# First attention block of a two-layer transformer kernel: order of the norm, the evictions, the value bias, the weight-chunk buffers and the bias row

## The reference, cut to what matters

```python
def _layernorm(x, axis=-1, eps=1e-05):
    m = jnp.mean(x, axis=axis, keepdims=True)
    v = jnp.var(x, axis=axis, keepdims=True)
    return (x - m) / jnp.sqrt(v + eps)

def _L0_attn_ref(x, Wqkv, bqkv, Wo, bo):      # x: 1 x 1024 x 512, d = 128
    qkv = jnp.einsum('bsc,cf->bsf', x, Wqkv) + bqkv
    q, k, v = ...                             # three parts of 128
    attn = jnp.einsum('bqd,bkd->bqk', q, k) / sqrt(d)
    attn = jax.nn.softmax(attn, axis=-1)
    out = jnp.einsum('bqk,bkd->bqd', attn, v)
    return jnp.einsum('bqd,dc->bqc', out, Wo) + bo

x = x + _L0_attn_ref(_layernorm(x), ...)
x = x + _L0_ffn_ref(_layernorm(x), w1, mean_w1, w2, mean_w2, w3, mean_w3)
```

## Time and profile before

| quantity | value |
|---|---|
| time, median of 3 runs | 1475.95 us (1475.61 to 1476.82) |
| time of the profiled execution | 1476.29 us |
| its span, first to last instruction | 1474.5 us |
| PE busy in the span | 1327.4 us (90%) |
| DVE, ACT, POOL busy | 1105.6 us (75%), 832.5 us (56%), 640.5 us (43%) |
| mean granted clock of PE | 0.954 |

### The profile page before, as it was taken

The page is one execution under the profiler, slowest core; times in us unless marked ns, Lnnn a source line. Parts: engine busy times, 40 slices in busy tenths (PEclk is TensorE's granted clock), DMA queues, the critical chain, the costliest instruction groups (busy, mean ns, idle before and its releaser), DMA issues.

```text
span 1474.5 us, 21228 instructions
## 1 busy us (share of the span) xinstructions
PE 1327.4 (90%) x7144; PEld 1105.3 (75%) x7144; DVE 1105.6 (75%) x2233; ACT 832.5 (56%) x1813; POOL 640.5 (43%) x629
## 2 busy tenths in 40 slices
PE   2777999999989789998659999999999999999977
PEld 1656788888789677776348888888888888888866
DVE  5637434433548599999969998898898998898864
ACT  4554442222236556774557767666676767667631
POOL 3421120000027445645556555655666555555522
PEclk9978999999999999998669999999999999999988
DMA  6531220000022334754820000000000000000101
GB/s 217 177 100 51 70 81 0 1 19 1 17 81 64 102 75 122 227 181 140 269 95 14 1 28 28 28 28 28 28 16 12 28 27 28 28 27 15 51 29 58
DMA packets 83722, 95.59 MB, mean 65 GB/s; under 512 B 11680, under 2 KB 59296, under 8 KB 83104
## 3 DMA queue, kind: packets, MB, share of 16 engines
q1 hardware_dynamic: 83616, 94.24, 20.2%
HBM read 75.34 MB, written 18.87 MB: 64 GB/s over the span
## 4 chain that ended last, share of the span: by engine, by line
PE 68%; DVE 18%; ACT 4%; issue 4%; DMA 2%; POOL 2%; SPq 1%; DVEq 1%; ACTq 0%; POOLq 0%
PE ps L328 16%; PE ps L330 15%; PE ps L329 15%; PE ps L1715 8%; PE ps L1735 3%; DVE acc L1299 3%; PE ps L1734 3%; DVE top L1310 2%; DVE xn_l L1361 1%; DVE rop L1322 1%; DVE acc L1313 1%; DVE rop L1320 1%; DVE pm L1349 1%; DVE rop L1321 1%; PE ps L1430 1%
## 5 line engine op out<-in xcount | busy, mean ns | idle before, releaser
L692 POOL TENSOR_SCALAR pm<-pm,smx 128x128 f32<-128x128 f32 (+7 forms) x256 | 190.5, 753 | 214.6 <-DVE smx L1355 214.6
L966 ACT ACTIVATE pm<-pm,smx 128x128 f32<-128x128 f32 (+7 forms) x256 | 197.2, 772 | 39.8 <-DVE smx L1349 38.7
L1349 DVE CUSTOM_DVE_ANT_0 pm<-ps,mbias 128x128 f32<-128x128 f32 (+7 forms) x256 | 191.3, 752 | 34.0 <-PE ps L1715 13.1
L1715 PE MATMUL ps<-ident,pm 128*128 128x128 f32 x1152 | 176.2, 278 | 9.0 <-DVE xn_l L1361 3.5
L972 ACT ACTIVATE xn_h<-ps 128x512 fp32r<-128x512 f32 (+3 forms) x256 | 128.8, 513 | 86.0 <-PE ps L1715 82.9
L1361 DVE TENSOR_TENSOR xn_l<-ps,xn_h 128x512 fp32r<-128x512 f32 (+3 forms) x256 | 144.6, 587 | 26.6 <-ACT xn_h L972 25.6
L328 PE MATMUL ps<-latT_l,qc_h 128*128 128x512 f32 (+3 forms) x384 | 143.1, 373 | 20.5 <-DVE smx L1349 12.5
L1715 PEld LDWEIGHTS ps<-ident,pm 128*128 128x128 f32 x1152 | 133.4, 142 | 35.3 <-issue 12.3
L330 PE MATMUL ps<-latT_h,qc_h 128*128 128x512 f32 (+3 forms) x384 | 134.1, 349 | 0.0
L329 PE MATMUL ps<-latT_h,qc_l 128*128 128x512 f32 (+3 forms) x384 | 133.4, 347 | 0.0
L1299 DVE SCALAR_TENSOR_TENSOR acc<-ps,iw,acc 128x768 f32<-128x768 f32 (+4 forms) x105 | 87.1, 876 | 23.5 <-ACT ps L865 23.3
(11 more groups left out here) (280 smaller groups left out, 3699.1 us busy)
## 6 DMA issues: line engine op xcount, KB each, us to landing
iwq_raw<-in_L_attn_idx_wq_w SPq DMA_DIRECT2D x48, 256.0 KB, 3.2
base<-in_L_ffn_mean_w SPq DMA_DIRECT2D x28, 256.0 KB, 2.8
wring<-in_L_ffn_w SPq DMA_DIRECT2D x24, 256.0 KB, 3.0
ow_raw<-in_L_attn_o_w SPq DMA_DIRECT2D x8, 512.0 KB, 3.9
xn_t<-in_L_attn_o_w SPq DMA_DIRECT2D x8, 512.0 KB, 4.0
wuvo<-pr_even SPq DMA_DIRECT2D x8, 512.0 KB, 4.9
wuvo<-pr_hl SPq DMA_DIRECT2D x8, 512.0 KB, 4.8
wuvo_h<-wuvo SPq DMA_DIRECT2D x16, 256.0 KB, 2.6
```

Source lines behind the costliest of these rows:

```text
L692: pool.tensor_scalar(pm[:, i % 4, 0:w], pm[:, i % 4, 0:w], smx[:, 32 + i:33 + i], 0.0, ALU.mult, ALU.add).then_inc(hd_p, 1)
L966: act.activation(pm[:, i % 4, 0:w], pm[:, i % 4, 0:w], ACT.Exp, bias=smx[:, i:i + 1], scale=-1.0, accum_out=smx[:, 16 + i:17 + i]).then_in ...
L1349: dve.tensor_tensor_reduce(out=pm[:, i % 4, 0:w], in0=two_banks(2 * (i % 2), w), in1=mbias[:, TRI[t]:TRI[t + 1]], scale=1.0, scalar=3.0 * BIG,
L1715: done = pe.transpose(ps[:, 4 + i % 2, tile(k)], pm[:, tq % 4, tile(4 * c + k)], ident[:])
```

## The change

- x is loaded on two semaphores (tiles 0 to 3, 4 to 7). `first_norm(half)` makes statistics, root and Newton steps for four tiles; the first half is scaled before the second half's statistics.
- Wqkv is split in four quarters between the tiles of the second half. The split of Wo (item W0) and the bias row (items B0, B4, into a buffer `bo_bc` of its own) come later, within the attention.
- The chunk ring has four buffers from the first chunk on.
- PE, ACT and DVE have lists of their own: `ATT_PE`, `ATT_ACT`, `ATT_DVE`. S0 and S1 come ahead of the products for v (items V0 to V7 of PE). On ACT the evictions T1 and T2 stand ahead of the exponentials S3 and S4, and so on; chunks are items C with a count.
- The bias of v is a matmul of a row of ones with the bias row, in float32, that opens the sum in PSUM (`value_tile`); ACT makes the high part, DVE the low part. v uses PSUM banks 6 and 7 in place of 4 and 5.
- The raw attention weights lie in a buffer of their own under `base2`, as do the split ones; SP waits at chunk 28, the first that overwrites them.

```diff
-    _slot = _c % 3 if _c < ROW_FREE else (_c - ROW_FREE) % 4
+    _slot = _c % 4
...
-ATT_ORDER = [(_step[0], int(_step[1:])) for _step in
-             "S0 S1 S2 T0 S3 T1 S4 T2 S5 T3 S6 O0 T4 Y0 Y1 S7 Y2 T5 Y3 T6 T7 O1 Y4 Y5 Y6 Y7".split()]
+ATT_PE = items("S0 S1 V0 V1 V2 V3 S2 V4 V5 V6 V7 T0 S3 T1 S4 T2 S5 T3 S6 O0 T4 S7 Y0 Y1 T5 Y2 T6 Y3 T7 O1 "
+               "Y4 Y5 Y6 Y7")
+ATT_ACT = items("S0 S1 C2 V0 C2 S2 C1 V1 T0 C1 T1 S3 T2 S4 C1 T3 S5 C1 S6 C3 O0 T4 C1 S7 T5 C1 T6 C1 T7 O1")
+ATT_DVE = items("S0 S1 W0 V0 S2 B0 V1 T0 S3 T1 S4 T2 S5 T3 S6 B4 O0 T4 S7 Y0 Y1 T5 Y2 T6 Y3 T7 O1 Y4 Y5 Y6 Y7")
...
-                sp.dma_start(xt(t), x_in[0, tile(t), :]).then_inc(ld_x, 16)
+                sp.dma_start(xt(t), x_in[0, tile(t), :]).then_inc(ld_x[t // 4], 16)
...
                 if chunk == 2 * NI:
-                    sp.wait_ge(at_w, 1)
+                    sp.wait_ge(at_w, 2)
+                    sp.wait_ge(at_proj, 6)
+                    sp.wait_ge(at_b, 2)
...
-            sqrt(0, NT)
-            for t in range(NT):
-                norm_hi(0, t)
-                if t >= 1:
-                    weight_chunk()
+            for half in range(2):
+                act.wait_ge(at_rv, half + 1)
+                c = slice(4 * half, 4 * half + 4)
+                act.activation(rs_sqrt[:, c], rs_var[:, c], ACT.Sqrt).then_inc(at_rs, 1)
+                for t in range(4 * half, 4 * half + 4):
+                    norm_hi(0, t)
+                    if t >= 3:
+                        weight_chunk()
+            for _ in range(4):
+                weight_chunk()
...
-                weight_chunk()
-            for _ in range(6):
-                weight_chunk()
+                if u < 2:
+                    weight_chunk()
+            for _ in range(3):
+                weight_chunk()
...
+            first_norm(0)
+            for t in range(4):
+                norm_scale(0, t)
+                if t >= 1:
+                    norm_lo(0, t - 1)
+            first_norm(1)
+            for t in range(4, NT):
+                norm_scale(0, t)
+                norm_lo(0, t - 1)
+                if t == 4:
+                    dve.wait_ge(ld_a, 80)
+                split(wqkv_h[:, t - 4, :], wqkv_l[:, t - 4, :], raw[:, t - 4, :])
+            norm_lo(0, NT - 1)
             dve.drain().then_inc(at_w, 1)
-            for t in range(NT):
-                dve.tensor_tensor(xt(t), xt(t), row_bc[:], ALU.add)
-            dve.drain().then_inc(row_free, 1)
...
+            def value_tile(t):
+                dst = ps[:, 6 + t // 4, tile(t % 4)]
+                pe.matmul(dst, ones[0:1, :], bv_bc[0:1, :], start=True, stop=False)
                 for k in range(NK):
-                    last = mm3(pe, ps[:, 4 + t // 4, tile(t % 4)], xn_h[:, k, tile(t)], xn_l[:, k, tile(t)],
-                               wqkv_h[:, k, tile(2)], wqkv_l[:, k, tile(2)], k == 0, k == NK - 1)
+                    last = mm3(pe, dst, xn_h[:, k, tile(t)], xn_l[:, k, tile(t)],
+                               wqkv_h[:, k, tile(2)], wqkv_l[:, k, tile(2)], False, k == NK - 1)
```

More of the change, by code:

```diff
@@ L73, in ds, with items @@
     return bass.ds(start, size)
-ATT_ORDER = [(_step[0], int(_step[1:])) for _step in
-             "S0 S1 S2 T0 S3 T1 S4 T2 S5 T3 S6 O0 T4 Y0 Y1 S7 Y2 T5 Y3 T6 T7 O1 Y4 Y5 Y6 Y7".split()]
+def items(order):
+    return [(step[0], int(step[1:])) for step in order.split()]
+ATT_PE = items("S0 S1 V0 V1 V2 V3 S2 V4 V5 V6 V7 T0 S3 T1 S4 T2 S5 T3 S6 O0 T4 S7 Y0 Y1 T5 Y2 T6 Y3 T7 O1 "
+               "Y4 Y5 Y6 Y7")
+ATT_ACT = items("S0 S1 C2 V0 C2 S2 C1 V1 T0 C1 T1 S3 T2 S4 C1 T3 S5 C1 S6 C3 O0 T4 C1 S7 T5 C1 T6 C1 T7 O1")
+ATT_DVE = items("S0 S1 W0 V0 S2 B0 V1 T0 S3 T1 S4 T2 S5 T3 S6 B4 O0 T4 S7 Y0 Y1 T5 Y2 T6 Y3 T7 O1 Y4 Y5 Y6 Y7")
 PE_ORDER = """T9 Q0+ S11 T10 V0 S12 T11 Q1+ T12 S13 T13 V1 T14 S14 T15 S15 T16 T17 V2 S0+ T18 T19 S1+ Q2+ T20 T21 S2+ S3+
@@ L286, in build @@
         rs_v, rs_s = sems("rs_", "v s")
-        at_w, at_proj, at_q, at_qkv, at_v = sems("at_", "w proj q qkv v")
+        at_rv, at_rs, at_w, at_proj, at_q, at_qkv, at_vhi, at_v, at_b = sems("at_", "rv rs w proj q qkv vhi v b")
         at_s, at_max, at_exp, at_tr, at_hi, at_lo = sems("at_", "s max exp tr hi lo")
@@ L761, in weight_down @@
                     .then_inc(ff_w2, 1)
-            for kind, i in ATT_ORDER:
+            for kind, i in ATT_ACT:
                 if kind == "S":
@@ L769, in _ @@
                     act.drain().then_inc(at_exp, 1)
-                    weight_chunk()
+                elif kind == "C":
+                    for _ in range(i):
+                        weight_chunk()
+                elif kind == "V":
+                    act.wait_ge(at_proj, 5 + i)
+                    act.activation(v_h[:, 4 * i:4 * i + 4, :], ps[:, 6 + i, :].rearrange("p (k s) -> p k s", k=4), COPY)\
+                        .then_inc(at_vhi, 1)
                 elif kind == "T":
@@ L1080, in _, with values @@
                 dve.drain().then_inc(at_qkv, 1)
-            for b in range(2):
-                dve.wait_ge(at_proj, 5 + b)
-                tmp = xn_t[:, b, :].rearrange("p (k s) -> p k s", k=4)
-                for i in range(4):
-                    dve.tensor_tensor(tmp[:, i, :], ps[:, 4 + b, tile(i)], bv_bc[:], ALU.add)
-                dve.drain()
-                split(v_h[:, 4 * b:4 * b + 4, :], v_l[:, 4 * b:4 * b + 4, :], tmp)
-                dve.drain().then_inc(at_v, 1)
+            def values(b):
+                dve.wait_ge(at_vhi, b + 1)
+                dve.tensor_tensor(v_l[:, 4 * b:4 * b + 4, :], ps[:, 6 + b, :].rearrange("p (k s) -> p k s", k=4),
+                                  f(v_h[:, 4 * b:4 * b + 4, :]), ALU.subtract).then_inc(at_v, 1)
             def means(m, a, b):
@@ L1113, in row_stats @@
                 dve.bn_stats(stats[:, 6 * i:6 * i + 6], xt(i))
-            for kind, i in ATT_ORDER:
+            for kind, i in ATT_DVE:
+                if kind == "V":
+                    values(i)
+                    continue
+                if kind == "W":
+                    split(wo_h[:], wo_l[:], attn_raw[:, NK * 3 * D0:])
+                    dve.drain().then_inc(at_w, 1)
+                    continue
+                if kind == "B":
+                    for t in range(i, i + 4):
+                        dve.tensor_tensor(xt(t), xt(t), bo_bc[:], ALU.add)
+                    dve.drain().then_inc(at_b, 1)
+                    continue
                 if kind == "O" and i == 1:
@@ L1438, in transposes_down @@
                 last.then_inc(ff_tr2, 1)
-            for kind, i in ATT_ORDER:
+            for kind, i in ATT_PE:
+                if kind == "V":
+                    value_tile(i)
+                    continue
                 if kind == "T" and i == 7:
@@ L1455, in _ @@
                     for c in range(2):
[L1456 to L1459 removed]
+                        reach(pe, at_lo, 2 * i + c - 1 if i else 0)
                         for k in range(4):
@@ L1479, in _ @@
                     pe.wait_ge(at_ot, i // 4 + 1)
+                    if i == 0:
+                        pe.wait_ge(at_w, 2)
                     if i >= 2:
```

77 lines of the change are left out of this document (35 added, 42 removed).

## The result

The changed kernel takes **1463.64 us** (median of 4 runs, 1461.96 to 1464.14) against 1476.38 for the kernel before (4 runs, 1475.61 to 1476.95): a ratio of 0.9912, 95% interval [0.9895, 0.9929]. It is faster, by 12.7 us where 28.0 were forecast, and it lies outside the range of 1443 to 1458. The profiled execution has a span of 1462.3 us (1474.5 before).

What follows compares the result with a forecast made beforehand. It took a closed ring of ACT and DVE, 6.15 us a round, to bound the score loop, and ACT afterwards. O1 moves from 127.49 to 99.5, a gain of 28.0: 1476.3 - 28.0 = 1448.3 us, range 1443 to 1458.

Steps and rivals of the forecast that it cites:

- Part 1: Start to projections: norm in halves, projections at 32.8 us against 42.85, with 1.75 us allowed for POOL's hits on DVE.
- Part 2: Projections to first exponential: S0 at 48.6, first exponential at 53.2 us against 72.30, after three chunks and the table load.
- a share only from T1 on: Allowance for PE's low clock from T1 to S6: between 0 and 6.9 us, taken as 1.4.
- Part 3: First exponential to O1, the second product with v: ACT becomes the bound; O1 at 98.1 us, 99.5 with allowance.
- a float32 128x128 product is two records, 8 x 2 x 0.11 = 1.8: PE's cost for the bias products in v's eight tiles, 1.8 us within PE's sum of 39.2.
- ACT's ledger: ACT's work from first exponential to O1: exponentials, evictions and chunks sum to 42.2 us, plus waits of 2.0 and 0.7.
- Rival A: First attention: PE's clock stays at mean 0.75, its 39.2 us become 52.3; O1 at 102.9, time 1451.7 us; chance 0.20.
- the same distances as before: Behind O1: same code in the same order, so the 28.0 us won ahead of it reach the end whole.

Runs made afterwards that it cites:

- the identity: Changed kernel with the value bias as a product of the 128x128 identity and the bias row on 128 partitions: 1449.14 us, second run 1451.34 us.
- no bias: Changed kernel with the value-bias product left out and nothing in its place: 1446.53 us.
- 32 rows: Changed kernel with the value-bias product over 32 rows in place of one, adding the bias 32 times: 1456.7 us, single run.
- the row twice: Changed kernel with the one-row bias product only ahead of v tiles 0 and 4, the other six without bias: 1448.94 us, single run.
- bias folded: Changed kernel with no bias in v; one product of bv and Wo between S1 and V0 is added to the output bias row: 1453.8 us.
- norm undivided: Kernel with the identity product, its first norm in one piece over eight tiles in place of halves: 1456.67 us.
- POOL held back: Kernel with the identity product; POOL's chunk 11 waits for the four q/k splits, and ACT takes two of three chunks later: 1452.94 us.

## Why the prediction was wrong, step by step

**Part 1: right in its outcome.** DVE's statistics start at 6.38 (forecast 6.1), the first reciprocal at 9.85 (9.55), the first scale at 11.07 (10.8), the projections at 33.46 (32.8). POOL took two long hits and some short ones, as provided for, one of them on the Newton steps of the second half, the other on a split:

```profile
22.35 1.21 DVE L1037 TENSOR_TENSOR rs_out<-rs_out,rs_tmp 128x4 f32<-128x4 f32 x1
...
31.07 1.60 DVE L1044 TENSOR_TENSOR wqkv_l<-attn_raw,wqkv_h 128x384 fp32r<-128x384 f32 x1
```

Late by 0.7.

**Part 2: right.** First exponential at 53.28 (53.2), carried by three chunks and the table load. S0 was later than put, 49.98 against 48.6, since I had given the q/k splits no share in the locks with POOL: three casts took 0.80, 0.90 and 0.99, and the last 1.29. ACT's chunks hid that. The low clock that I had given a share only from T1 on was there at S0 and S1 already: they took 4.26 us (49.98 to 54.24) where the second run of the identity has 2.86 at the high clock (50.81 to 53.67), and ACT waited 1.35 us for the maximum of S1.

**Part 3: the failed step** is the term "a float32 128x128 product is two records, 8 x 2 x 0.11 = 1.8". I sized a product with one row by the record of one of 128x128, the only float32 product I had looked at, and by the pitch of the fp32r matmuls. It took 0.56 at the high clock, 8 x 0.56 = 4.5, and it pulled the clock down, which made the twelve matmuls of a tile last some 2.6 in place of 1.36 in four of the eight tiles, and drew out S2 between the halves and T0 and S3 behind v as well. I had taken the product as a cost and not as something that the trace of before did not contain; an operation that the trace does not show needs a bound from both sides, and this one got a single value.

The accounts close. The profiled execution took 1464.1 against a forecast of 1448.3: 13.7 us of the 15.8 are O1's, 2.1 lie behind it (below). Of the 13.7, 0.7 is the later start of the projections. From the first tile of v to O1 the row costs 11.9 to 12.2 us more than the identity. Of these 8 x (0.56 - 0.20) = 2.9 is the length of the product, and the rest the clock: 4 tiles x (3.48 - 1.92) = 6.2, S2 2.80 in place of 1.45, T0 1.58 in place of 0.82 and S3 2.26 in place of 1.46, in all 9.1. The remaining 0.8 to 1.1 us are no matter of the product: S0 came 1.4 us late and ran in part at the low clock before the first bias product (part 2).

**ACT's ledger: right.** With PE at its clock, ACT was busy 39.0 us of the 44.7 between the first exponential and O1, in the kernel without the bias; 42.2 had been put for its work, gaps between its instructions included, and 2.7 for waits. With the identity this stretch is 46.4 and 47.9 us, where 99.5 - 53.2 = 46.3 had been forecast. In the changed kernel ACT was not the bound: PE was, for two stretches, of 5.3 and 6.8 us.

**Rival A had the right engine and the wrong reason.** It gave O1 at 102.9 for a mean clock of 0.75; the stage from the first exponential to O1 had 0.78. But I looked for the low clock where PE rests between rounds, put it on a sum of 39.2, and found "PE rests less now, which speaks against it". In v, where it cost most, it fell while PE never rested; only the fall at S0, at 51.5 us, came behind a rest. And A let ACT's work run on beside PE's; in truth v stands in a row with the loop, since in PE's list T0 comes behind V7, and ACT's next evictions wait for it. So what v with S2 lost, 24.55 - 14.19 = 10.4 us, was lost at O1 in full.

**Behind O1**: "the same distances as before" was right to a few us only. From O1 to the end of the span:

| kernel | O1 | span | rest |
|---|---|---|---|
| before | 127.49 | 1474.5 | 1347.0 |
| after | 113.19 | 1462.3 | 1349.1 |
| identity, first and second run | 102.13, 100.38 | 1446.3, 1447.0 | 1344.2, 1346.6 |
| no bias | 96.72 | 1442.5 | 1345.8 |
| 32 rows | 109.20 | 1454.9 | 1345.7 |
| the row twice | 102.15 | 1447.2 | 1345.1 |
| bias folded | 104.02 | 1453.2 | 1349.2 |
| norm undivided | 105.62 | 1452.9 | 1347.3 |
| POOL held back | 102.92 | 1455.2 | 1352.3 |

That code is the same in all but the first, and its length varies by 8 us. The granted clock from 600 to 800 us varies with it only in part: 0.86 in both runs with the identity and in the changed kernel, 0.85 with the bias folded, 0.84 without the bias and with the norm undivided, 0.82 with POOL held back. What makes it longer or shorter was not found. Each row is one execution, and executions of one kernel differ as much: the norm undivided took 1452.76 to 1462.09 us. No difference of 1 to 3 us between these kernels should be read as an effect of their edits.

**What is left is a better kernel.** With the identity in place of the row the change gives 1449.14 and 1451.34 in its two sessions, 24 to 25 us less than the kernel before beside it, and beats both kernels. That is 1 to 3 us above the forecast, 1448.3, for a kernel that differs by the operands of one instruction from the one that was forecast.

## What to carry to other kernels

Look at every instruction that a change adds and ask whether the trace has that very form, rows and type and all; a product "of the same size" is not the same if its contraction is one row deep. To add a bias inside a chain of matmuls on TensorE, use full-height operands (the identity, and the bias spread over the partitions, if it is there anyway), or leave the addition to an engine with slack, and look at the granted clock beside the busy share: 100% busy at a clock of 0.66 is a third of the stage gone. And when an engine is found waiting, ask which engine will have to do the work that was moved, before moving it.

## What the runs showed of the hardware

- **TensorE's granted clock can fall while TensorE is never idle.** In the kernel before the change, with one-row products it went from 1.00 to 0.50 in the midst of a stretch of 100% busy time, and stayed there to the end of v; with 128-row products in the same places it stayed at 1.00. The Trainium skill (TensorE: Matmul & The Clock Gate, "What's actually happening") says that the gate goes by how busy the engine has been of late. The busy share of the records is not that measure: here it was the same, 100%, in both kernels.
- **Few rows are not cheap rows.** The float32 pair took 0.56 us of PE's time with one row, 1.90 - 1.36 = 0.54 with 32, and 0.20 with 128, all at the high clock. The Trainium skill (TensorE: Matmul & The Clock Gate, "Why this matters for your kernels") has a single matmul of 32 rows cost the same as one of 128. The durations nearly agree (0.48, 0.48, 0.44), the time until the next matmul starts does not.
- **A rest does not fix the clock either.** Rests of 3.17 and 3.27 us ahead of S0 were followed by a granted clock of 0.66 and of 1.00 in the stretch from 50 to 55 us.
- **The clock column can miss a low clock.** In the kernel before, it says 1.00 from 44 to 48 us, but the projections' matmuls of 512 columns stand 0.43 apart there (44.27, 44.70), as they do in the changed kernel at 51.55 and 51.98, where the column says 0.50, and 0.23 apart from 48.5 on (48.76, 48.99). Why, the runs don't show; the distance between matmuls is to be read beside it.
- **POOL and DVE.** A cast of 128x512 takes 0.43 us alone and up to 1.29 beside a subtraction of POOL; in the kernel in which POOL is held back all four took 0.43. The Newton step that took 0.16 in the first half (10.82) took 1.21 in the second (22.35), beside a subtraction of POOL from 22.29 on.
